# A new written-out order of work, and two counters in place of one, in a two-layer transformer kernel

## The reference

```python
# layer 0: adaptive layer norm, causal attention, MLP
mod = silu(cond) @ Wada + bada                       # shift, scale, gate, twice
xm  = layernorm(x, g1, be1) * (1 + sc_a) + sh_a
x   = x + gt_a * (softmax(mask(q k^T / sqrt(16))) v @ Wproj + bproj)
xm  = layernorm(x, g2, be2) * (1 + sc_m) + sh_m
x   = x + gt_m * (gelu(xm @ W1 + b1) @ W2 + b2)
# layer 1: layer norm with gamma, beta from the vector; attention without mask
h   = gamma * layernorm(x) + beta
h1  = x + (softmax(q k^T) / sqrt(256)) v @ Wp.T + bp
out = gamma * layernorm(h1) + beta + h1
```

## Time and profile before

| what | value |
| --- | --- |
| median of 3 runs | 1254.23 us (1252.0 to 1255.34) |
| span of the profiled execution | 1249.3 us |
| PE busy | 1168.6 us (94%) |
| DVE busy | 850.9 us (68%) |
| ACT busy | 678.2 us (54%) |
| DMA engines | 24.9% of their time |

### The profile page before, as it was taken

How to read it: one execution, slowest core, us unless ns; L and a number is a source line. 1 busy time by engine, 2 the same in 40 slices (tenths; PEclk the granted TensorE clock), 3 DMA queues, 4 the chain that set the end, 5 groups by cost and what they waited for, 6 DMA issues and landing times.

```text
span 1249.3 us, 18813 instructions
## 1 busy us (share of the span) xinstructions
PE 1168.6 (94%) x6604; PEld 591.7 (47%) x6604; DVE 850.9 (68%) x1779; ACT 678.2 (54%) x1346; POOL 279.0 (22%) x378
## 2 busy tenths in 40 slices
PE   7888989999899998999899999999989999999995
PEld 4434644464444644555344644446445553445332
DVE  4735498637886579836887378855788368754775
ACT  1272145656557465565555565564655656543673
POOL 1133022311332023311233013320243002310003
PEclk9898999999999999999999999999999999989998
DMA  5603031301432032500524024310425005200311
GB/s 177 192 2 102 2 112 41 111 12 65 117 87 69 19 109 74 135 4 19 149 52 118 2 73 109 100 57 18 113 69 137 1 2 162 39 17 25 91 33 42
DMA packets 59191, 89.36 MB, mean 72 GB/s; under 512 B 12914, under 2 KB 23762, under 8 KB 59098
## 3 DMA queue, kind: packets, MB, share of 16 engines
q1 hardware_dynamic: 58078, 87.35, 24.9%
q10 hardware_dynamic: 1020, 0.81, 0.2%
HBM read 24.41 MB, written 4.70 MB: 23 GB/s over the span
## 4 chain that ended last, share of the span: by engine, by line
PE 59%; DVE 20%; ACT 6%; SPq 5%; DMA 5%; issue 3%; POOL 1%; ACTq 0%; DVEq 0%; POOLq 0%
PE X L1034 13%; DVE MX L760 10%; PE OP L942 10%; PE X L1083 9%; PE X L1059 9%; PE SC L953 8%; PE X L972 8%; SPq L412 4%; ACT E L619 3%; DMA OC<-OE 2%; DVE STAT L769 2%; DMA QS<-NT 2%; DVE XN L812 1%; DVE XR L878 1%; DVE TMP L874 1%
## 5 line engine op out<-in xcount | busy, mean ns | idle before, releaser
L760 DVE TENSOR_REDUCE MX<-X 128x1 f32<-128x512 f32 (+3 forms) x1024 | 533.4, 581 | 187.6 <-PE X L975 100.0
L619 ACT ACTIVATE E<-SC 128x512 f32<-128x512 f32 (+3 forms) x1024 | 459.8, 525 | 323.6 <-PE SC L953 258.1
L972 PE MATMUL X<-KS,QS 96*128 96x512 bf16 (+3 forms) x1024 | 296.6, 346 | 10.7 <-DVE MX L760 6.4
L953 PE MATMUL SC<-QS,KS 99*128 99x512 bf16 (+3 forms) x1024 | 276.3, 342 | 24.9 <-ACT E L619 15.9
L942 PE MATMUL OP<-E,V 128*32 128x512 f32 (+3 forms) x2048 | 207.6, 523 | 6.2 <-ACT OE L634 5.4
L953 PEld LDWEIGHTS SC<-QS,KS 99*128 99x128 bf16 x1024 | 93.3, 97 | 176.0 <-ACT E L619 112.4
L972 PEld LDWEIGHTS X<-KS,QS 96*128 96x128 bf16 x1024 | 97.5, 98 | 160.5 <-DVE MX L760 51.2
L537 POOL TENSOR_SCALAR_AFFINE_SELECT E<-E 128x512 f32<-128x512 f32 x128 | 86.8, 680 | 252.4 <-ACT E L619 252.4
L1083 PE MATMUL X<-XT,W 128*128 128x512 f32 x256 | 123.8, 618 | 2.1 <-ACT XT L652 2.1
L1059 PE MATMUL X<-XT,WQKV 128*128 128x512 f32 x256 | 117.0, 602 | 1.5 <-ACT XT L652 1.5
L1034 PE MATMUL X<-W,HID 128*128 128x256 f32 x512 | 115.3, 380 | 0.4 <-ACT HID L672 0.4
(11 more groups left out here) (92 smaller groups left out, 920.4 us busy)
## 6 DMA issues: line engine op xcount, KB each, us to landing
QS<-PART SPq DMA_DIRECT2D x192, 128.0 KB, 2.4
KS<-PART SPq DMA_DIRECT2D x192, 128.0 KB, 2.5
OC<-OE SPq DMA_DIRECT2D x56, 128.0 KB, 3.9
RB<-recip_sums SPq DMA_DIRECT2D x56, 128.0 KB, 2.6
XIN<-in_x SPq DMA_DIRECT2D x8, 512.0 KB, 5.0
ROW<-row_vectors SPq DMA_DIRECT2D x8, 512.0 KB, 3.6
out<-OUT SPq DMA_DIRECT2D x7, 512.0 KB, 3.4
W<-in_w SPq DMA_DIRECT2D x2, 1024.0 KB, 6.7
```

The lines of the kernel that those rows point to most:

```text
L619: a.activation(E[:, at["tick"].index() % 3, j, lo:T], SC[(at["head"].index() + j) % 3][:, lo:T], ACT.Exp, scale=HD ** -0.5 if layer == 0 e ...
L760: v.reduce_max(MX[:, qt, h:h + 1], X[at["bank"].index() % BANKS][:, 0:w], AX.X, negate=True)\
L953: t_.matmul(SC[(at["head"].index() + j) % 3][:, lo:T], KS[stacks(layer, b)][0:ALL_ROWS, h, kt * P:kt * P + P], QS[stacks(layer, b)][0:ALL_ ...
L972: ins = t_.matmul(bank[:, 0:w], QS[stacks(layer, b)][0:CUT_ROWS, h, qt * P:qt * P + P], KS[stacks(layer, b)][0:CUT_ROWS, h, 0:w], start=Tr ...
```

## The change

Three edits.

1. The lists `HEAD`, `RING` and `TAIL` are written anew. The tokens are the same, and so is the number of instructions, but for table loads.
2. `dense_done` becomes `dense_act` and `dense_dve`, each with a count of its own (`by_act`, `by_dve`), and the wait of one engine for the other's evictions goes.
3. Where an instruction has several waits, the one that is expected to be met last is written first. The compiler leaves the wait written first on the instruction itself and puts the others ahead of it as instructions that only wait.

```diff
-        dense_done = sem("dense_done")
+        dense_act = sem("dense_act")
+        dense_dve = sem("dense_dve")
...
                     for j in ((0, 1, 2), (3,))[half]:
+                        wait(act, head_full, at["head"].at(1, j + 1))
                         if j == 0:
-
                             wait(act, pv_done, at["tick"].at(1, -2))
-                        wait(act, head_full, at["head"].at(1, j + 1))
                         a.activation(E[:, at["tick"].index() % 3, j, lo:T],
...
                 def bank(k):
-                    if k == 0:
-
-                        wait(act, dense_done, c.at())
                     wait(act, dense_full, c.at(1, k + 1))
...
 RING = """
-    row0 s stackq1 a s p o a stackk1 s s t s s s p s s pack1 s a s o s s s p s s a s s s p s s a s s s p o s
-    nm0b s s recip1 a max0b s s s p s a s p s s t s a s o s s p s a s scale1 s p o row1 a s t s p proj1 a s s p
...
+    row0 s a s p s s s s a s s s o t pack1 s s p s s s a s stackq1 stackk1 s p recip1 s o s a s s s p s a s
+    row1 s s s p o nm0b a s s p s s s a p t scale1 max0b a s s o s p s s a s s s p o t a s s s p s proj1
...
```

More of the change, by code:

```diff
@@ L59 @@
 HEAD = """
[L60 to L69, removed]
@@ L81 @@
-TAIL = """
[L82 to L91, removed]
+    stat_a norm_a mods turn_a q0 k0 stackq0 stackk0 rows v0 s s s s s s s s s s s s s s s s s s s s s s
@@ new lines @@
+    nm0_0 max0_0 s s s s s s s row0 s s a s nm0_1 p s s s s a s s max0_1 s p s s s s a s s p o a s s s p s
+    a o t p keep0 s s s nm0_2 a s p s s stat_a a p max0_2 s s s a o p norm_a s s a o t p s s s s nm0_3 a
+    fold0_0 p a p max0_3 turn_a a o p a fold0_1 p o t a fold0_2 p a p o a p q0 o t fold0_3 merge0 stackq0
+    proj0 k0 stackk0 norm_m v0 turn_m up_0 s s up_1 s s s s s s up_2 s s up_3 s s up_4 s s s s s s up_5 s s
+    up_6 s s s s s s up_7 s s s s s s nm0a down_0 down_1 s max0a down_2 s s s down_3 a p row0 keep0 s s s a
@@ new lines @@
+TAIL = """
+    s stackq1 o t s a s s p row0 keep0 s s s a s s s p s s s a s stackk1 pack1 p s o s s a s s p s recip1 a
+    s s s s p o t nm0b s s a s s p max0b s a o scale1 p s s a s s p a o t row1 p s s s a s s p s a s p o a
+    s s p s a s s p s o t s a s s p s s a s p s o a s s nm1a s p proj1 max1a o t pack0 s s s recip0 v1 a s
+    s s gain1 p scale0 a s s p o a close1 hold1 proj0 s s norm_m p s a s p o a p turn_m s a s s s s p up_0
+    s s a up_1 up_2 up_3 up_4 up_5 t up_6 up_7 s s p s s down_0 down_1 down_2 down_3 s s norm_1 s a o p s o
+    t turn_1 s s s s nm1b q1 max1b k1 a stackq1 p row1 a p o stackk1 s a s s p s s s a s s p o t s a s s p
+    s s s a s p s nm1_0 s o s a s s s s p s a s s p o t s s max1_0 v1 pack1 a s p s s s a s p s s a s s p
+    nm1_1 max1_1 s a s s s s o p s s s s a o t s p s s recip1 a p s s s nm1_2 a max1_2 p o a s s s p o t a
+    s s s s p s a p s o a s s p s s scale1 nm1_3 a fold1_0 p o t max1_3 proj1 gain1 row1 a p a p close1
+    hold1 fold1_1 a o p a fold1_2 p o t fold1_3 merge1 proj1 gain1 close1""".split()
@@ L124 @@
 ADDS["norm_m"]["bias"] = 1
+BY_ACT = ("turn_a", "turn_m", "turn_1", "merge0", "merge1") + tuple(f"up_{_n}" for _n in range(FT))
 for _n, _adds in ADDS.items():
@@ L130 @@
           "rows1", "x_in", "gain", "close", "stack0", "stack1", "high", "low", "norm", "head", "tick",
-          "step", "masked", "group", "scan", "halves", "fold", "bank")
+          "step", "masked", "group", "scan", "halves", "fold", "bank", "by_act", "by_dve")
 class Count:
@@ L654, in work @@
                                      bias=FM[:, (first + 1) * KT + ft, bass.ds(b, 1)])\
-                            .then_inc(dense_done, 1)
+                            .then_inc(dense_act, 1)
                 elif what in ("q0", "k0", "q1", "k1"):
                     side = "qk".index(what[0])
-                    for half in range(2):
-                        wait(act, stack_dma[0][half], at["stack0"].at(192))
-                        wait(act, stack_dma[1][half], at["stack1"].at(192))
                     for t in range(2):
-                        part = PART[:, side, 0, t, :]
+                        part, psum = PART[:, side, 0, t, :], bank(t)
+                        if t == 0:
+                            for half in range(2):
+                                wait(act, stack_dma[0][half], at["stack0"].at(192))
+                                wait(act, stack_dma[1][half], at["stack1"].at(192))
                         if what[1] == "0":
-                            ins = a.activation(part, bank(t)[:], ACT.Copy)
+                            ins = a.activation(part, psum[:], ACT.Copy)
                         else:
-                            ins = a.activation(part, bank(t)[:], ACT.Identity,
+                            ins = a.activation(part, psum[:], ACT.Identity,
                                                bias=BQK1[:, 2 * side + t:2 * side + t + 1])
@@ L677, in work @@
                     for kt in range(KT):
-                        a.activation(OC[:, kt, :], bank(kt)[:], ACT.Copy).then_inc(dense_done, 1)
+                        a.activation(OC[:, kt, :], bank(kt)[:], ACT.Copy).then_inc(dense_act, 1)
                 elif what.startswith("max"):
@@ L1070, in work @@
                     if grouped(n, b):
[L1071 removed]
+                        wait(pe, dense_act, at["by_act"].at())
                     else:
@@ L1106, in work @@
                 elif what.startswith("max"):
+                    wait(pe, max_pool, at["maxima"].at(4, 4))
                     psum = bank(0).bitcast(BF16)
@@ L1109, in work @@
                     rows = 3 * (heads.stop - heads.start)
-                    wait(pe, max_pool, at["maxima"].at(4, 4))
                     for qt in range(TT):
```

110 lines of the change are left out of this document (62 added, 48 removed).

## The result

The changed kernel takes **1361.6 us** (median of 4 runs, 1359.23 to 1363.01); the kernel before, on the same chip in the same session, 1253.24 (4 runs, 1252.0 to 1255.34). The ratio is 1.086, 95% interval 1.083 to 1.089. The forecast was 1329, with 1278 to 1362 as its range: the direction is right, the loss of 108 us was forecast as 75, and the median lies 0.4 us inside the upper end of the range, one of the four runs (1363.01) outside it. The profiled span is 1357.5 us, 108.2 longer than before.

A forecast was written before the change was run, and what follows sets the result against it. PE was taken as the bound on average, DVE's scans between `k1` and `proj1`. Ring +68, TAIL +11, clock +12, fewer loads and waits -12, HEAD -4: +75 on 1249.3, span 1324, plus 4.9: 1329 us, range 1278 to 1362.

The forecast's parts named there:

- What bounds: PE, busy 1168.6 of 1249.3 us; between the end of `k1` and `proj1` DVE's scans set the pace.
- Scan 24: First layer-1 scan of a ring pass: PE stands some 9.8 us for stack DMAs, until T+23.1 (T: `k1`'s end).
- `scale1` and `proj1`: In a ring pass DVE stands 7.5 us for `RB`; `proj1` comes 16.6 us later; net +13.6 a pass, +68.
- Rival B: Only the wait before scan 24 is paid, none at `scale1`: 7.2 us a pass, 1286 us; chance 0.13.
- Clock: Half clock after each long wait, mostly hidden by DVE's pace: 2 us a pass, +12 over six passes.
- Outside the stretch: Beyond `k1` to `proj1`: 3.0 us of PE's work moved out; fewer loads and waits gain 2 a pass, -12.
- HEAD: Before the ring passes: first maxima cut 4.5 us earlier, modulation products delay the start by perhaps 1; taken as -4.
- TAIL: SP stands at `keep0`, `RB` lands late, `scale1` stands at scan 29, `proj1` comes near T+54: +11.
- C: Faster: SP gets through the stack in under about 6 us and scan 24 finds its data; 1232 us, chance 0.09.
- D: No difference: the waits are paid but the rest of the pass gives some 13 us back; 1254 us, chance 0.04.

The follow-up runs named there:

- pack_first: lists_old with only SP's order in RING as in the changed kernel (`stackq1` and `stackk1` right behind `pack1`): 1283.45 us, +43.5 against lists_old.
- scale_late: The changed kernel with `scale1` in RING moved from behind the 31st scan to behind the 40th: 1339.8 us, ratio 1.070 to the kernel before.
- lists_old: The changed kernel with all three lists of before, keeping the new counters and order of waits: 1239.96 us, ratio 0.987 to the kernel before.
- head_old: The changed kernel with HEAD alone taken back to the list of before: 1348.59 us, ratio 1.074 to the kernel before.
- tail_old: The changed kernel with TAIL alone taken back to the list of before: 1347.96 us, ratio 1.074 to the kernel before.
- stack_back: The changed kernel with `stackq1` and `stackk1` ahead of `pack1` again in RING, everything else as changed: 1334.6 us, ratio 1.065 to the kernel before.
- exp_wait_old: lists_old with the two waits of the first exponential of a step in the old order: 1246.01 us, ratio 0.992 to the kernel before.

## Why the prediction was right, and where its sizes were off

*What bounds.* Right: PE stayed the bound, and the stretch behind `k1` was the place. From T to T a pass grew by 15.8 us: this stretch by 19.0, and the rest became 3.2 shorter.

*Scan 24.* Right, and well sized: the forecast was T+23.1 after a wait of 9.8; measured T+24.4 after 8.9. The steps hold one by one: ACT's copy was put at T+9.6 and `pack1` leaves at T+10.1; the 12 stack DMAs were to be out at T+21.2 and are at T+22.5, the first six taking 4.6 us instead of 3.8.

*`scale1` and `proj1`.* Right: T+37.2 for `RB` and T+44.2 for `proj1` were forecast, T+37.8 and T+45.9 measured. pack_first and scale_late show the two waits apart: 8.7 us a pass for the first alone, 4.4 for taking away the second. Rival B, one wait only, fell with the 34.6 us for `RB`.

*Clock.* 2 us a pass on top of T+44.2 was the term; the stretch ended 1.7 after it. The clock was at or near half in the windows behind the standstill shown, and no run held the waits and took the clock away, so its share is argued, not shown. The Trainium skill, "TensorE: Matmul & The Clock Gate", section "HAM oscillation — how this bites in real kernels", says that a wait for a DMA in each round drops the clock each time, so that the next stretch starts cold. The trace agrees: the granted clock was 0.50 inside each of the five standstills before scan 24 and in the 3 to 8 us behind each (on which the forecast leaned, stand at a wait of 2.1 us for ACT and not for a DMA).

*Outside the stretch: a step that failed.* I took -3.0 of moved work and -2 of gain for each pass, -5.0; it was -3.2. The moved work is there: PE is busy 3.3 us less in the second window. The gain is not: PE's idle time in it was 2.7 us and is 2.8. Edits 2 and 3 do gain, 13 us over the program, but lists_old's pass is 144.4 against 145.2, so 0.8 a pass; the new list gave that back. Five times 1.8 is 9 of the 33 us missed.

*HEAD: wrong in sign.* Forecast -4, measured +13 (head_old), +10.0 by the trace. I counted scans ahead of the cut and not what the products of `mods` stand for: their weights' landing, 3.63 us, then 10.4 us for 48 matmuls that took 5.7 when they came later, all ahead of `turn_a`. I put 1 us on it. I also did not follow POOL, whose stand at the gate row is 13.27 us where it was 6.46. With 14 us of difference this is the largest part of the miss.

*TAIL.* Forecast 11, with clock and gain cancelling; +19.2 by the trace, +13.6 by tail_old. The size is too small by 3 to 8 us, and the place was wrong. `RB` was nearly in time (DVE waits 1.29 us for it), and the wait is earlier, at `recip1`, where DVE's timeline has

```profile
1150.72 0.55 DVE L904 RECIPROCAL RR<-RS 128x64 f32<-128x64 f32 x1 [9.79 <-DMA RS<-OE]
...
1160.18 1.22 DVE L908 TENSOR_TENSOR OC<-OC,RB 128x1024 f32<-128x1024 f32 x1 [1.29 <-DMA RB<-recip_sums]
```

`k1` ends at 1121.7 there, so `proj1` starts at T+57.9 where T+54 was forecast. I had passed over `recip1` in the sum, the same omission that made my expectation of stack_back miss.

*The sum.* HEAD +14, outside the ring stretch +9, TAIL +8, inside the ring stretch +2 (19.0 a pass measured where 16.6 and 2 of clock were forecast): the 33 us missed. The ring terms that I worked out step by step hold to about 2 us a pass; the two that I estimated without following an engine through them, both as gains, were a loss and nothing.

*Luck.* The 79 us of the ring passes came by the waits that were forecast, so the direction is no accident. That the time fell inside the range is one in part: the upper end, 1362, stood for 5 us of clock a pass and no gain elsewhere, and it was nearly reached by HEAD and TAIL instead. A pass of 161.3 us lies just above the 155 to 161 that I had named.

*C and D.* C needed SP to be done with the stack in under 6 us; it took 16.5. The Trainium skill, "DMA: Bandwidth & Descriptors", section "Anatomy of one DMA — SWDGE (gpsimd) path", lays the fixed cost of a DMA on its completion. It says so of DMAs that GpSimd issues, and these come from SP, so it could not carry C. Here SP's own 0.6 us for each issue, in one queue, is what decides, and pack_first prices a change in nothing but that order at 43.5 us. D failed: the rest of the pass gave 3.2 and not 13.

## What to carry to other kernels

Read the engine that only issues as you read the ones that compute: 24 issues at 0.64 us are 15 us of an in-order queue, and what stands behind them can be worked out to a microsecond or two from one timeline. Where a block of transfers has a part that is needed at once and a part that is not, split it, and put the urgent small things between the halves. In a hand-written order a token's place is good or bad only together with the places it waits for: undoing one move can uncover a wait as long as the one removed (10.3 us at `recip1` in stack_back), so price every wait on the new path before moving anything, and follow the engines through the places that look like gains as well.

## What was not expected of the hardware

- A table load hides in a wait if the wait that is met last stands on the instruction itself. The idle time ahead of 40 loads went from 30.7 to 5.3 us with no load less, and swapping two waits back brought 15.5 of it back (exp_wait_old). I had given this no price of its own.
- PE ran its first products at half the later speed, up to 17.0 us before and up to 29.9 us now, while the clock column of the profile said 1.00. This accounts for the same 48 narrow matmuls having taken 10.4 us (7.00 and 3.56 us in the rows) where they come first and 5.7 (3.63 and 2.21) ten microseconds later. What kept the speed down for longer was not tried.
